# One scale for each gate and up row half in place of two, and the first row's front ahead of the last fills, in a cross-attention and FP4 feed-forward kernel

## The reference

```python
def fp4_quant_dequant(x):                     # BLOCK = 16, last dimension
    xb = x.reshape(shape[:-1] + (shape[-1] // BLOCK, BLOCK))
    scale = jnp.maximum(jnp.max(jnp.abs(xb), axis=-1, keepdims=True) / 6.0, 1e-12)
    xn = xb / scale
    idx = jnp.searchsorted(_MID, jnp.abs(xn))
    return (_GRID[idx] * jnp.sign(xn) * scale).reshape(shape)
def fp4_linear(x, w):
    return jnp.einsum('bsk,nk->bsn', fp4_quant_dequant(x), fp4_quant_dequant(w))
x = x + xattn(layernorm(x), ctx, ctx, mask, Wq, bq, Wk, bk, Wv, bv, Wo, bo)
h = silu(fp4_linear(layernorm(x), w_gate)) * fp4_linear(layernorm(x), w_up)
x = x + fp4_linear(h, w_down)                 # x: 4 x 2048 x 512; w_gate, w_up: 1408 x 512
```

## Time and profile before

| what | value |
|---|---|
| time, median of 3 | 2022.99 us (2022.44 to 2023.09) |
| time of the profiled execution | 2019.79 us |
| its span | 2017.9 us |
| mean granted PE clock | 0.974 |
| PE busy | 1894.5 us, 94% |
| DVE busy | 1758.7 us, 87% |
| ACT busy | 1266.9 us, 63% |
| POOL busy | 446.9 us, 22% |

### The profile page before, as it was taken

One profiled execution on the slowest core, in us unless ns is written; L12 is line 12 of the kernel. 1 busy time (PEld: TensorE's weight loads), 2 busy tenths in 40 slices (PEclk: granted clock), 3 DMA queues, 4 the chain that ended last, 5 costly groups with the idle time before them and its releaser, 6 DMA issues.

```text
span 2017.9 us, 48669 instructions
## 1 busy us (share of the span) xinstructions
PE 1894.5 (94%) x17724; PEld 1189.1 (59%) x17792; DVE 1758.7 (87%) x2676; ACT 1266.9 (63%) x2613; POOL 446.9 (22%) x526
## 2 busy tenths in 40 slices
PE   6447899999999999999999999999999999999987
PEld 4334556665666666665666566666666666656643
DVE  7897888899889888988889988988898888988864
ACT  4675676666666676667666766666666766676421
POOL 5662122112211222112211221122112221122100
PEclk8768999999999999999999999999999999999998
DMA  5355665665566566655666657655665566565623
GB/s 171 111 126 101 122 129 136 150 135 131 135 150 136 126 133 143 148 124 132 142 149 128 132 129 153 133 129 132 152 138 125 133 142 148 125 132 127 131 55 85
DMA packets 716996, 265.34 MB, mean 131 GB/s; under 512 B 667930, under 2 KB 669878, under 8 KB 716958
## 3 DMA queue, kind: packets, MB, share of 16 engines
q1 hardware_dynamic: 715374, 264.85, 59.4%
q10 hardware_dynamic: 1584, 0.01, 0.1%
HBM read 66.34 MB, written 34.86 MB: 50 GB/s over the span
## 4 chain that ended last, share of the span: by engine, by line
PE 85%; DVE 6%; DMA 3%; issue 2%; POOL 1%; SPq 1%; ACT 1%; DVEq 0%; POOLq 0%; another core or an unknown queue 0%; ACTq 0%
PE psum L725 43%; PE psum L661 37%; PE psum L738 2%; PE psum L767 2%; DMA t_room<-halves 1%; SPq L346 1%; PE psum L756 1%; POOL h_room L561 1%; DVE h_room L1321 1%; DVE psum L1259 1%; POOL h_room L565 1%; DVE h_room L1279 1%; DMA ph_room<-h_room 1%; DMA q_room<-in_L_xattn_Wk_dram 0%; DVE wguT L1247 0%
## 5 line engine op out<-in xcount | busy, mean ns | idle before, releaser
L725 PE MATMUL psum<-wguT,t_room 128*128 128x352 bf16 x6144 | 942.7, 314 | 17.3 <-DVE h_room L1427 9.1
L725 PEld LDWEIGHTS psum<-wguT,t_room 128*128 128x128 bf16 x6144 | 597.3, 98 | 348.0 <-DVE h_room L1427 10.5
L661 PE MATMUL psum<-wdT,ph_room 128*128 128x512 bf16 x2108 | 469.9, 381 | 11.1 <-DMA ph_room<-h_room 10.9
L582 POOL TENSOR_TENSOR ln_var_eps<-ln_mean_var,eps 128x1 f32<-128x1 f32 x128 | 103.8, 811 | 1184.2 <-DVE ln_mean_var L1395 995.7
L661 PEld LDWEIGHTS psum<-wdT,ph_room 128*128 128x128 bf16 x2112 | 207.5, 98 | 263.4 <-issue 17.6
L983 ACT ACTIVATE silu_g<-psum 128x352 f32<-128x352 f32 x256 | 117.4, 459 | 379.9 <-PE psum L725 376.7
L989 ACT ACTIVATE probs<-psum,neg_max 128x77 f32<-128x77 f32 x1024 | 244.3, 350 | 3.7 <-DVE neg_max L1433 3.0
L1427 DVE TENSOR_TENSOR h_room<-silu_g,psum 128x352 f32<-128x352 f32 x256 | 132.2, 517 | 81.1 <-ACT silu_g L983 81.1
L1020 ACT ACTIVATE t_room<-psum,bq_col 128x128 bf16<-128x128 f32 x256 | 72.9, 367 | 186.3 <-PE psum L661 186.3
L661 PE MATMUL psum<-t_room,wqT 128*128 128x128 bf16 x3072 | 187.4, 222 | 0.8 <-DMA t_room<-halves 0.7
L661 PEld LDWEIGHTS psum<-t_room,wqT 128*128 128x128 bf16 x3072 | 177.5, 100 | 1.4 <-DMA t_room<-halves 1.0
(11 more groups left out here) (110 smaller groups left out, 2479.4 us busy)
## 6 DMA issues: line engine op xcount, KB each, us to landing
io_room<-in_x_dram SPq DMA_DIRECT2D x128, 256.0 KB, 2.8
x_scratch<-x_new SPq DMA_DIRECT2D x64, 256.0 KB, 2.0
x_cur<-x_scratch SPq DMA_DIRECT2D x64, 256.0 KB, 3.3
out_dram<-io_room SPq DMA_DIRECT2D x64, 256.0 KB, 2.4
t_room<-halves SPq DMA_TRANSPOSE x192, 3.2
raw<-in_L_ffn_w_down_dram SPq DMA_DIRECT2D x4, 704.0 KB, 4.2
raw<-in_L_ffn_w_gate_dram SPq DMA_DIRECT2D x11, 256.0 KB, 2.7
raw<-in_L_ffn_w_up_dram SPq DMA_DIRECT2D x11, 256.0 KB, 3.0
```

The lines of the kernel that those rows point to most:

```text
L582: own.did(pool.tensor_tensor(var_eps, mean_var[:, 1:2], eps[:], ALU.add))
L661: ins = pe.matmul(dst, left(i), right(j), start=first and n == 0, stop=last and n == len(PRODUCTS) - 1)
L725: ins = pe.matmul(ps[:, 0:CW], left[:, i, kc, :], wguT[:, which, j, kc, cols], start=(kc == 0 and i == j), stop=(kc == KC - 1 and i == LO))
```

## The change

Three things are done. First, the scale of a gate or up half is computed once: `scale` writes straight to `w_sc[:, half, 1]` for rows of even number and `w_sc[:, half, 3]` for odd ones, and both the inverse and POOL's multiplication read it there. `result_scale` stays for w_down alone. Second, the fills go round by `bank[(n + 2) % 8]`, so that bank 6 is last used by fill 36 in place of fill 38. Third, `weight_front(0)` moves from behind the last fill to in front of the bias fill (fill 37) in DVE's list, with a wait for the 37 fills before. `weight_front` also gets a wait for `w_quant` of the row before last.

```diff
+        def fill_bank(n):
+            return bank[(n + 2) % 8]
...
-            def weight_end(half, width, at, *hq_free):
+            def weight_end(half, width, at, scale_row, *hq_free):
...
                 own.did(pool.tensor_tensor(blocks(hq[:, cols]), blocks(hs[:, cols]),
-                                           spread(w_sc[:, half], 3, width // FP4_BLOCK), ALU.mult), w_quant, at)
+                                           spread(w_sc[:, half], scale_row, width // FP4_BLOCK), ALU.mult), w_quant, at)
...
             def gate_up_end(i, half):
-                weight_end(half, D, 2 * i + 2 * KC + half + 1, *((w_ps, 2 * i - 1 + half) if i else ()))
+                weight_end(half, D, 2 * i + 2 * KC + half + 1, 2 * (i % 2) + 1, *((w_ps, 2 * i - 1 + half) if i else ()))
...
-                ps = bank[n % 8]
+                ps = fill_bank(n)
...
             def scale(job):
 
                 own.after(marks[job.name])
-                step_of(job, dve.tensor_scalar(job.sc[:, 1, 0:job.nb], job.sc[:, 0, 0:job.nb], 1.0 / 6.0,
+                step_of(job, dve.tensor_scalar(job.scale_row[:, 0:job.nb], job.sc[:, 0, 0:job.nb], 1.0 / 6.0,
                                                SCALE_FLOOR, ALU.mult, ALU.max))
...
-                step_of(job, dve.reciprocal(job.sc[:, 2, 0:job.nb], job.sc[:, 1, 0:job.nb]))
+                step_of(job, dve.reciprocal(job.sc[:, 2, 0:job.nb], job.scale_row[:, 0:job.nb]))
...
-            def weight_job(name, scales, cols, divided, squared, done):
+            def weight_job(name, scales, parity, cols, divided, squared, done):
                 part = [t[:, cols] for t in (raw, hv, h_sq, hm, hs, hq)]
+                scale_row = w_sc[:, name, 1] if parity is None else w_sc[:, name, 2 * parity + 1]
...
-            def weight_sum(job, before):
+            def weight_sum(job, before, own_scale=True):
 
                 at_least(dve, w_quant, before - 1 + job.name)
-                result_scale(job)
+                if own_scale:
+                    result_scale(job)
                 dve.wait_ge(*job.squared)
                 own.did(dve.tensor_tensor(job.tot, job.mag, job.val, ALU.subtract), *job.done)
 
+            def weight_front(i):
+
+                dve.wait_ge(w_loaded, 32 * i + 16 * KC + 32)
+                at_least(dve, w_quant, 2 * (i - 2) + 2 * KC + 2)
+                weight_start(gate_up_jobs(i), 2 * i + 2 * KC)
...
+                if kind == "bias":
+                    dve.wait_ge(prep_lo, n)
+                    weight_front(0)
...
-            def weight_front(i):
-
-                dve.wait_ge(w_loaded, 32 * i + 16 * KC + 32)
-                weight_start(gate_up_jobs(i), 2 * i + 2 * KC)
-
             def weight_end(i, half):
-                weight_sum(gate_up_jobs(i)[half], 2 * i + 2 * KC)
+                weight_sum(gate_up_jobs(i)[half], 2 * i + 2 * KC, own_scale=False)
...
-            dve.wait_ge(prep_lo, len(fills))
-            weight_front(0)
             first_norm(0)
```

More of the change, by code:

```diff
@@ L29, in at_least @@
         eng.wait_ge(sem, value)
-Job = namedtuple("Job", "name source src val sq mag tot res sc nb divided squared done")
+Job = namedtuple("Job", "name source src val sq mag tot res sc scale_row nb divided squared done")
 class Steps:
@@ L259, in blocks, with spread_row @@
             return t.rearrange("p (b k) -> p b k", k=FP4_BLOCK)
+        def spread_row(row, nb):
+            return row[:, 0:nb].unsqueeze(2).to_broadcast([P, nb, FP4_BLOCK])
         def spread(sc, row, nb):
-            return sc[:, row, 0:nb].unsqueeze(2).to_broadcast([P, nb, FP4_BLOCK])
+            return spread_row(sc[:, row], nb)
         def existing(t):
@@ L565, in weight_end @@
                 own.did(pool.tensor_tensor(blocks(hq[:, cols]), blocks(hs[:, cols]),
-                                           spread(w_sc[:, half], 3, width // FP4_BLOCK), ALU.mult), w_quant, at)
+                                           spread(w_sc[:, half], scale_row, width // FP4_BLOCK), ALU.mult), w_quant, at)
             for i in range(KC):
                 for half in range(2):
-                    weight_end(half, HALF, 2 * i + half + 1,
+                    weight_end(half, HALF, 2 * i + half + 1, 3,
                                *((prep_ps, fills.index(("down", (i - 1, half + 1))) + 1) if i else ()))
@@ L1292, in rescale, with weight_jobs @@
                 own.after(marks[job.name])
-                step_of(job, dve.tensor_tensor(blocks(job.res), blocks(job.tot), spread(job.sc, 1, job.nb), ALU.mult),
+                step_of(job, dve.tensor_tensor(blocks(job.res), blocks(job.tot), spread_row(job.scale_row, job.nb), ALU.mult),
                         job.done)
-            def weight_job(name, scales, cols, divided, squared, done):
+            def weight_job(name, scales, parity, cols, divided, squared, done):
                 part = [t[:, cols] for t in (raw, hv, h_sq, hm, hs, hq)]
-                return Job(name, None, *part, scales[:, name], (cols.stop - cols.start) // FP4_BLOCK,
+                scale_row = w_sc[:, name, 1] if parity is None else w_sc[:, name, 2 * parity + 1]
+                return Job(name, None, *part, scales[:, name], scale_row, (cols.stop - cols.start) // FP4_BLOCK,
                            divided, squared, done)
-            def weight_jobs(scales, width, before):
-                return [weight_job(s, scales, slice(s * width, (s + 1) * width),
+            def weight_jobs(scales, parity, width, before):
+                return [weight_job(s, scales, parity, slice(s * width, (s + 1) * width),
                                    *((sem, before + (s + 1)) for sem in (w_val, w_grid, w_sum)))
@@ L1327, in _ @@
                     dve.wait_ge(w_loaded, 16 * (what + 1))
-                    weight_start(weight_jobs(w_sc, HALF, 2 * what), 2 * what)
+                    weight_start(weight_jobs(w_sc, None, HALF, 2 * what), 2 * what)
                     continue
                 if kind == "round":
-                    for job in weight_jobs(w_sc, HALF, 2 * what):
+                    for job in weight_jobs(w_sc, None, HALF, 2 * what):
                         weight_sum(job, 2 * what)
                     continue
+                if kind == "bias":
+                    dve.wait_ge(prep_lo, n)
+                    weight_front(0)
                 if kind == "keys" and what == 0:
```

10 lines of the change are left out of this document (5 added, 5 removed).

## The result

The changed kernel took 2016.5 us (median of 10) beside 2022.07 us for the kernel before in the same session (median of 10, 2017.69 to 2023.99). Three slow executions (2215.28 us of the changed kernel, later 3319.28 and 3320.42) are left out of the ratios, and without its own the changed kernel has a median of 2016.31 us (2014.35 to 2017.16). The profiled execution took 2015.32 us with a span of 2013.5 and a mean clock of 0.975, against 2019.79, 2017.9 and 0.974, which is 4.47 us less.

A forecast was written before the change was run, and what follows sets the result against it. PE bounds the pipeline, so only its start moves, set by a DVE-chain prologue. Terms of 3.1 + 0.1 + 1.0 = 4.2 us took the timed median from 2022.99 to 2018.8 us, range 2016.4 to 2021.6.

The forecast's parts named there:

- signs of being wrong: Last fill after 68.9 us, subtraction of 1.3 us or more in rows 1, 3, 5, 9, or pipeline start moved without its end.
- rival B: Prologue: DVE is the path everywhere, both idle times and all 22 scales gained, 6.4 us, time 2016.6; chance 0.08.
- What bounds the kernel: Whole kernel: PE bounds the pipeline, so the change only moves its start, through a prologue that is a DVE chain.
- Part 1: Front of row 0 moved into DVE's idle time ahead of the last fills: norm of tile 0 3.09 us earlier.
- Bring nothing more: Rows 0 and 1: idle times of 0.39 and 0.70 us go without gain, since tile 1's norm waits for its load.
- part 3: Prologue rows: 22 scale instructions removed from DVE, nine on the path at 0.10 us plus 0.1, 1.0 us gained.
- Part 2: SBUF port at the bias fill: POOL first gives +0.3 us, DVE first -0.3; taken as 0.1 us.
- the count of nine scales on the path: Three in rows 2, 4 and 10, six in rows 3, 5 and 9, each worth 0.10 us.
- rival A: Prologue: all scale savings absorbed by waits for ACT, POOL's port or loads; gain 3.1 to 3.3 us, 2019.8; chance 0.16.
- Rival D: Paired subtractions: POOL takes the port first, costing 1.2 us per row; seven rows 2027.2, one row gain 3.0; chance 0.07.
- Rival C: Pipeline entry: SP's transposes and the p_h load give back half of the 4.2 us, time 2020.9; chance 0.13.

The follow-up runs named there:

- the repeat: The changed kernel run again unaltered in a later session: 2016.15 us, ratio 0.9979 to the kernel before.
- PE kept busy: Matmuls of zeros added where PE waits at the pipeline's entry: kernel before 2019.02 us (0.9995), changed kernel 2016.16 us (0.9981).
- front only: Kernel before with only the front of row 0 moved and the banks turned by two, both scales kept: 2016.73 us, ratio 0.9978.
- the two with one back: One removed scale put back ahead of row 1's first subtraction: in the changed kernel 0.9973, in the kernel with only the scales changed 0.9993.
- the norm end moved: Changed kernel with first_norm_end(1) later in DVE's list: behind both subtractions 0.9969, behind gate_up_low(0, 0) 0.9976, the latter with zero matmuls added 0.9967.
- scales only: Changed kernel with banks and front of row 0 as before: 2019.98 us, ratio 0.9988; again, 2018.9 us, 0.9994.
- banks only: Kernel before with only the banks of the fills turned by two: 2020.94 us, ratio 0.9998.

## Why the prediction was right in sum and wrong in its parts

The forecast was a gain of 4.2 us and a time of 2018.8, in a range of 2016.4 to 2021.6. The time was 2016.5, the gain 5.0 (3.2 to 6.9); the repeat gave 4.2, and the change with PE kept busy 3.8, both against the kernel before. Not every term came out. That the time lies in the range is in part luck. It is 0.1 us above the lower end, the 2016.31 of the result and the repeat's 2016.15 are below it, and the traces put the change itself at 2.9 us. What the profiles show beyond that up to the pipeline came from PE's clock, 1.0 us in the fills and 1.3 us at the entry. One of the signs of being wrong came true as well: a subtraction of 1.75 us in row 1. The chances had a slip: "a little over half" of 0.56, with rival B's 0.08, is about 0.4 and not 0.50. Whether the gain is beyond 0.2% the interval leaves open (0.9984 at its upper end).

**What bounds the kernel: right.** The change acted on the prologue alone, and the first gate and up matmul and the end moved by nearly the same amount, 3.9 and 4.4 us.

**Part 1, 3.1 us: right, a little low.** The front ran under POOL's work on w_down block 3, and the last fill was not delayed by it. That tile 1's load sets its norm held. Its issue came 3.67 us behind the norm of tile 0 in place of 3.87, and the load took 2.3 us in the change, 2.7 in its repeat and 2.4 in "front only", so the norm gained 0.6 us beyond the 3.1 in the change and 0.3 in the repeat, where it waited 0.47 us for the tile:

```profile
73.39 0.69 DVE L1404 BATCH_NORM_STATS2 ln_stats<-io_room 128x6 f32<-128x512 f32 x1 [0.47 <-DMA io_room<-in_x_dram]
```

The low half behind it evened that out: it meets POOL and took 1.37 us in the change, 1.03 in the repeat and 0.94 before. So row 2's front stands 11.2 us behind L in both. What failed are two steps. "Bring nothing more" was a little too low, and the 0.39 of waiting for ACT did not go, as this part had it, but stayed (0.41), as part 3 had it. The part comes to 3.3 to 3.5.

**Part 2, 0.1 us: right within its bounds.** POOL came first, the case that was priced at +0.3. Its block 3 took 6.90 us where it took 7.22 before. The moved front didn't slow down beside POOL's instruction of 61.06 (1.26 us for the two divisions, as before). That is what the Trainium skill says in "SBUF — State Buffer", section "Who interferes with whom", of DVE instructions with at most one SBUF input, and the trace agrees.

**Part 3, 1.0 us: wrong, and in the traces with the opposite sign.** The term was mis-sized in two ways. First, the count of nine scales on the path. From the front of row 3 to the first matmul, where eight of the nine stood, the kernel before takes 80.6 us in both of its profiles. The eight profiles with all the scales gone take 80.1 to 80.8 us, and the two with one back 79.7 and 80.4. That is 0.2 us less on average where 0.8 was counted. So DVE's 0.1 us per scale are mostly absorbed further on. Where, the traces don't separate: the front of row 7 of the changed kernel waits 0.61 us for its load of weights, but "front only", with its scales, waits 0.53 us there too. That is rival A. In row 2 0.25 us are gained, where 0.1 was counted. Second, row 1. Rival D's mechanism happened exactly there, the one row that the prediction named for it, at the price that it gave: 1.75 against 0.68 us, or with the scales that had been there 1.2 us on the path. The rival was right that this would be in one row at most, and had left its cost out of the sum. What it had not seen is which side moves. DVE's second subtraction could not become earlier, since it starts 0.1 us after ACT's rounding step ends, before and after (81.18 and 81.26; 76.47 and 76.58). POOL's could: its last rstd instruction ends 0.12 to 0.14 us behind DVE's first subtraction in all traces with the norm end unmoved, and against ACT's step that first subtraction starts 0.1 us earlier, since the scale ahead of it is gone. So POOL's subtraction starts 0.06 us ahead of DVE's and not 0.07 behind it. That it hangs on this one instruction is shown: the loss is there in the five profiles with all scales gone and the norm end unmoved, in none of the four with the scales kept, in none of the three with the norm end moved, and in none of the two with that one scale back. Part 3 comes to 0.25 + 0.1 - 1.2, or about -0.8. That is what the traces show up to the first matmul. The timed ratios of "scales only" do not confirm it: they stand for gains of 0.6 to 4.2 us and of -0.6 to 3.0 us, and both leave out a loss of 0.8, the second barely.

**Rival B** (everything on the path) had the time that is nearest to the measured one, 2016.6, but fell by the traces, since the gain from L is 2.6 and not 6.4. **Rival C** (half given back at the entry) fell: the distance grew there, with the 72 matmuls at 10.91 in place of 12.21 us. **Rival D** in its form of a single row had put the gain at 3.0 us, which is what the traces give.

**The sum.** By the traces the change is worth 3.4 + 0.3 - 0.8 = 2.9 us, and both kernels kept busy at the entry are 2.9 us apart in their medians. The timed 5.0, 4.2 and 3.8 lie above that. The interval of the first (3.2 to 6.9) doesn't hold it, those of the two others (2.4 to 6.1 and 2.0 to 5.7) do. The time of the prediction, 2018.8, was made against a median of 2022.99 from three executions; in the later sessions the kernel before had 2022.07, 2021.44, 2019.9 and 2020.4.

**What stays open.** Two things. "Scales only" has a longer prologue by 0.9 us in both of its profiles, and yet its medians lie 1.5 us below those of the kernel before in both sessions (0.9988 and 0.9994). Of this the entry could give 1.3, since both profiles had 10.91 us there where the kernel before had 12.21; whether its timed executions had that too no row tells. At the tile near 1829 us its two profiles are 0.6 and 0.7 us ahead of the kernel before. A part could also lie in the slow load of tile 0, which "front only" and "banks only" had. And the change is timed at 1 to 2 us more than its traces show. PE's clock in the fills may be behind it: the low stretch at 36 to 42 us is missing in one of the six profiles of kernels without the moved front, and in five of the eight with it. But that stretch lies 18 us ahead of the moved front, and fourteen single profiles don't tell a cause from chance. The two ends of the pipeline scatter by 3.7 and 2.9 us from profile to profile besides, whatever the kernel, and with that the question was not settled.

## What to carry to other kernels

Work moved into an idle stretch of the engine that ends last was worth its full length here, and what stands behind it should be followed to the next load and that load's issue. Small instructions taken off a full engine were mostly not worth their count, as later waits ate them; and where two engines' instructions on a shared port follow each other within 0.1 us, taking one away can turn their order and cost ten times what it saves. After such a change, look in the trace for an instruction that takes about 1 us more than its twins, and see whether one cheap instruction or another order turns it back.

## What the runs showed of the hardware

The order at the port hung on 0.06 to 0.07 us where the records keep the two starts apart, and came out the same way in both profiles of each kernel that was run twice. The loser's record covers its wait: 1.75 against 0.68 us on DVE, 1.73 to 1.78 against 1.26 on POOL. So POOL loses about 0.5 us where DVE loses 1.1. DVE was the engine that ended last here, so it was POOL that should wait. Instructions of 128x1 meet the port as well: the first of POOL's rstd took 0.67 us in the kernel before, in row 0, and 0.19 in row 1 of the change (75.33).

PE's clock differs from profile to profile at the same place of nearly the same program: 10.91, 12.2 to 12.6 or 13.85 us for the same 72 matmuls after waits of 2.5 to 2.7 us, and 10.91 in all three kernels in which PE had products of zeros to do in these waits. That saved up to 1.3 us in the trace, but the time of the kernel before changed by no more than the measurement can tell (0.9995, 0.9986 to 1.0004).
